# A graph-convolution kernel on one core: the order of the panels in its last step, the place where d is turned, and the order of its loads

## What is computed

```python
h = jnp.maximum(_layernorm(x, axis=-1), 0.0)
rowsum = adj.sum(axis=1)
d_inv_sqrt = jnp.where(rowsum > 0, rowsum ** (-0.5), 0.0)
normalized_adj = d_inv_sqrt[:, None] * adj * d_inv_sqrt[None, :]
support = normalized_adj @ h
out = support @ W + b
x = x + jax.nn.relu(out)
```

## Time and profile before

| | us |
|---|---|
| runs, median of 3 | 409.94 (409.82 to 417.97) |
| profiled execution, its time | 411.25 |
| profiled execution, its span | 409.2 |
| TensorE busy | 390.9 (96%) |
| VectorE busy | 311.0 (76%) |
| ScalarE busy | 292.1 (71%) |
| GpSimd busy | 115.7 (28%) |

### The profile page before, as it was taken

The page is one execution under the profiler, slowest core; times in us unless marked ns, Lnnn a source line. Parts: engine busy times, 40 slices in busy tenths (PEclk is TensorE's granted clock), DMA queues, the critical chain, the costliest instruction groups (busy, mean ns, idle before and its releaser), DMA issues.

```text
span 409.2 us, 5151 instructions
## 1 busy us (share of the span) xinstructions
PE 390.9 (96%) x1760; PEld 324.3 (79%) x1760; DVE 311.0 (76%) x314; ACT 292.1 (71%) x285; POOL 115.7 (28%) x271
## 2 busy tenths in 40 slices
PE   3999799999999999999999999999999999999991
PEld 3888687888888888888888888888888888887771
DVE  5757668878797878869585987869386987929996
ACT  2799868887888888597776778876677793445622
POOL 3343525242422362332132521433023360000000
PEclk9999999999999999999999999999999999999997
DMA  8999999999999999999999989999899991097656
GB/s 286 424 418 362 421 421 422 422 419 421 420 422 422 419 420 421 400 388 425 420 421 361 356 315 389 422 421 422 322 336 360 343 362 70 24 400 295 202 170 243
DMA packets 22472, 147.39 MB, mean 360 GB/s; under 512 B 2608, under 2 KB 2864, under 8 KB 6064
## 3 DMA queue, kind: packets, MB, share of 16 engines
q1 hardware_dynamic: 22448, 147.07, 90.0%
HBM read 142.87 MB, written 4.19 MB: 359 GB/s over the span
## 4 chain that ended last, share of the span: by engine, by line
PE 69%; DMA 12%; DVE 7%; issue 5%; ACT 5%; SPq 1%; ACTq 0%; DVEq 0%
PE moved L685 17%; PE moved L686 17%; PE moved L687 17%; DMA at<-in_adj_t 6%; DMA nat<-in_adj 6%; PE held L685 5%; PE held L686 5%; PE held L687 5%; PE moved L655 3%; DVE acc L551 2%; DVE lo L536 1%; DVE acc L566 1%; DVE nat L572 1%; ACT hi L352 1%; ACT G L364 1%
## 5 line engine op out<-in xcount | busy, mean ns | idle before, releaser
L352 ACT ACTIVATE hi<-at,s 128x1024 fp32r<-128x1024 f32 x112 | 123.0, 1146 | 46.6 <-issue 33.3
L532 DVE SCALAR_TENSOR_TENSOR lo<-at,s,hi 128x1024 fp32r<-128x1024 f32 x112 | 141.1, 1279 | 17.9 <-ACT hi L352 17.9
L685 PE MATMUL moved<-hi,G 128*128 128x512 f32 x384 | 150.1, 391 | 3.0 <-DVE acc L548 2.1
L686 PE MATMUL moved<-lo,G 128*128 128x512 f32 x384 | 149.5, 389 | 0.0
L687 PE MATMUL moved<-hi,G 128*128 128x512 f32 x384 | 149.4, 389 | 0.0
L551 DVE TENSOR_TENSOR acc<-moved,acc 128x1024 f32<-128x1024 f32 x84 | 102.7, 1223 | 53.3 <-PE moved L687 53.2
L339 ACT ACTIVATE nat<-nat 128x2048 f32<-128x2048 f32 x64 | 122.3, 1912 | 12.1 <-DMA nat<-in_adj 12.1
L685 PEld LDWEIGHTS moved<-hi,G 128*128 128x128 f32 x384 | 72.1, 188 | 20.5 <-DVE acc L551 3.2
L687 PEld LDWEIGHTS moved<-hi,G 128*128 128x128 f32 x384 | 72.1, 188 | 15.1
L686 PEld LDWEIGHTS moved<-lo,G 128*128 128x128 f32 x384 | 72.1, 188 | 14.6
L462 POOL TENSOR_TENSOR row_sum<-part 128x1 f32<-128x1 f32 x32 | 16.4, 511 | 170.5 <-ACT nat L339 170.4
(11 more groups left out here) (57 smaller groups left out, 228.4 us busy)
## 6 DMA issues: line engine op xcount, KB each, us to landing
nat<-in_adj SPq DMA_DIRECT2D x64, 1024.0 KB, 10.3
at<-in_adj_t SPq DMA_DIRECT2D x64, 1024.0 KB, 10.6
nat<-in_x_t SPq DMA_DIRECT2D x6, 512.0 KB, 4.1
out<-nat SPq DMA_DIRECT2D x5, 512.0 KB, 5.1
at<-in_x SPq DMA_DIRECT2D x4, 512.0 KB, 5.6
turned<-in_x SPq DMA_DIRECT2D x3, 512.0 KB, 14.1
turned<-in_x_t SPq DMA_DIRECT2D x2, 512.0 KB, 5.2
out<-turned SPq DMA_DIRECT2D x2, 512.0 KB, 5.0
```

The source lines that it names most:

```text
L352: nc.scalar.activation(hi[g % RING][:, 2 * c:2 * c + 2, :], at[g % LA][:, 2 * c:2 * c + 2, :], ACT.Copy, scale=s[:, j:j + 1]).then_inc(hi_ ...
L532: nc.vector.scalar_tensor_tensor(out=lo[g % RING][:, tiles, :], in0=at[g % LA][:, tiles, :], scalar=s[:, j:j + 1], in1=hi[g % RING][:, til ...
L685: nc.tensor.matmul(into[:, f, :], big, hi[g % RING][:, t, :], start=begins, stop=False)
L686: nc.tensor.matmul(into[:, f, :], big, lo[g % RING][:, t, :], start=False, stop=False)
```

## The change

The last step takes the panels in the order 2 to 7, 0, 1, so that both held panels come last. d is turned one step earlier, in step 13, two quarters each within panels 0 and 1 (slot 52), and ScalarE copies it in its loop 52. SP's loop g loads slot g + 3 instead of g + 2, with slot 2 ahead of the loops. The table of row blocks adds one for every 8 slots instead of 13, so `make_G` comes up to two slots earlier. The first chunk of x is loaded in two halves, with a mean for each. In the opening TensorE turns chunk 1 after it has projected chunk 0; ScalarE sums row block 0 before it copies chunk 1; VectorE copies chunks 3 and 4 from PSUM, and centres each chunk before it takes the next one's statistics. x comes back in LX = 4 buffers, and the sum of the first position goes to `acc` like the others.

The core of the diff (left out: declarations of names, `take_stats`, `centre` and `mean_of`, which take the first chunk in halves, and the wait in `project`, which asks `turned_signal`):

```diff
-    return [0] + list(range(HELD, NP)) + [1] if k == LAST else list(range(NP))
+    return list(range(HELD, NP)) + list(range(HELD)) if k == LAST else list(range(NP))
...
-        end = min(2 * WIDTHS[0] + min(2 * (g + 1), g + 3) + g // 13, 2 * NB)
+        end = min(2 * WIDTHS[0] + min(2 * (g + 1), g + 3) + g // 8, 2 * NB)
...
-    LX = 3
+    LX = 4
...
         def x_out(pos):
             e = pos % LX
-            flat = nat[2][:, e * BW * D:(e + 1) * BW * D] if e < 2 else turned[1][:, :]
+            flat = nat[2][:, e * BW * D:(e + 1) * BW * D] if e < 2 else turned[e - 2][:, :]
...
         def total(pos):
-            if pos == 0:
-                return turned[0][:, :].rearrange("p (f r) -> p f r", r=PW)
-            return acc[:, (pos - 1) % (NP - HELD), :, :]
+            return acc[:, pos % (NP - HELD), :, :]
...
+        def turned_signal(c):
+
+            if c in BY_VECTOR:
+                return hT_late, BY_VECTOR.index(c) + 1
+            return hT_ready, c + 1 - sum(b < c for b in BY_VECTOR)
...
-                if pos == 0 and k == LAST:
-                    for q in range(NP // 2):
+                if pos < HELD and k == LAST - 1:
+                    for q in range(2 * pos, 2 * pos + 2):
                         use(("d_row", q), (gathered + q) % ROT, d_row_ready, q + 1)
...
@@ block.sync
-            load_x(0)
+            half = BW // 2
+            sp.dma_start(h(0)[:, 0:half, :], x[0][:, 0:half, :]).then_inc(x_first, DMA)
+            sp.dma_start(h(0)[:, half:BW, :], x[0][:, half:BW, :]).then_inc(x_landed[0], DMA)
             load_x(1)
...
             load_slot(0)
             load_slot(1)
+            load_slot(2)
             sp.dma_start(b_sb[:, :], b).then_inc(b_landed, DMA)
...
-                if g + 2 < len(SLOTS):
-                    load_slot(g + 2)
+                if g + 3 < len(SLOTS):
+                    load_slot(g + 3)
@@ block.scalar
             take_turned(0)
+            sum_nat(0)
             take_turned(1)
-            sum_nat(0)
             round_raw(0)
+            take_turned(2)
             sum_nat(1)
-            take_turned(2)
             sum_nat(2)
             round_raw(1)
-            take_turned(3)
             sum_nat(3)
             round_raw(2)
-            take_turned(4)
             round_slot(0)
...
+                if k == LAST - 1 and q == 0:
+                    for r in range(NP // 2):
+                        take_d_rows(r)
                 if k == LAST:
                     if q == 0:
                         act.wait_ge(b_landed, DMA)
-                        for r in range(NP // 2):
-                            take_d_rows(r)
@@ block.gpsimd
+            def mean_of_first():
+                pool.wait_ge(stats_made, BW // 2)
+                then(nc.gpsimd.tensor_tensor(out=mean2[:, 0:BW // 2], in0=stats[:, 0:BW // 2, 1],
+                                             in1=stats[:, 0:BW // 2, 4], op=ALU.add))
+                nc.gpsimd.tensor_scalar(minus_mean[:, 0:BW // 2], mean2[:, 0:BW // 2], -0.5, None,
+                                        ALU.mult).then_inc(mean_first, 1)
...
-            mean_of(0)
+            mean_of_first()
+            mean_of(0, BW // 2)
             mean_of(1)
+            mean_of(2)
             rstd_of(0)
-            mean_of(2)
@@ block.vector
+            def take_turned(c):
+                dve.wait_ge(h_turned, c + 1)
+                dve.wait_ge(hW_done, c - 1)
+                nc.vector.tensor_copy(hT(c), pair_of(("turn", c))[:, :, :]).then_inc(hT_late, 1)
...
-                if pos == NP - 1:
+                if i < HELD:
                     dve.wait_ge(out_ready, pos - (NP - HELD) + 1)
-                elif i < HELD:
-                    dve.wait_ge(panel_done, NP * LAST + pos + 1)
+                    if pos < NP - 1:
+                        dve.wait_ge(panel_done, NP * LAST + pos + 1)
...
             take_stats(0)
+            centre(0)
             take_stats(1)
-            centre(0)
             centre(1)
             take_stats(2)
+            centre(2)
             take_stats(3)
-            centre(2)
             centre(3)
+            rest_of_raw(0)
             take_stats(4)
-            rest_of_raw(0)
             centre(4)
+            take_turned(3)
             rest_of_raw(1)
+            take_turned(4)
             rest_of_raw(2)
@@ block.tensor
-                    if pos == 0 and c < WIDTHS[k] - 1 and f == FD - 1:
-                        amid(k, c)
+                    if pos < HELD and c == 0 and f == FD - 1:
+                        amid(k, pos)
...
-            def amid(k, c):
+            def amid(k, pos):
...
-                if k == LAST and c >= 1:
-                    turn_d(2 * c - 2)
-                    turn_d(2 * c - 1)
+                if k == LAST - 1:
+                    turn_d(2 * pos)
+                    turn_d(2 * pos + 1)
...
             turn(0)
-            turn(1)
             pe.wait_ge(w_landed, DMA)
             project(0)
+            turn(1)
             turn(2)
```

More of the change, by code:

```diff
@@ L34 @@
 AHEAD = 5
+BY_VECTOR = [3, 4]
 TURNED_IN = {5: 5, 6: 7, 7: 10}
@@ L212, in build @@
         consts_made = sem("consts_made")
+        x_first = sem("x_first")
+        mean_first = sem("mean_first")
         stats_made = sem("stats_made")
@@ L218, in build @@
         hT_ready = sem("hT_ready")
+        hT_late = sem("hT_late")
         hW_done = sem("hW_done")
@@ L247, in use @@
             over[pair] = (signal, count)
+        def turned_signal(c):
+            if c in BY_VECTOR:
+                return hT_late, BY_VECTOR.index(c) + 1
+            return hT_ready, c + 1 - sum(b < c for b in BY_VECTOR)
         for c in range(AHEAD):
-            use(("turn", c), c % ROT, hT_ready, c + 1)
+            use(("turn", c), c % ROT, *turned_signal(c))
         use(("project", AHEAD - 1), AHEAD % ROT, raw_ready, AHEAD)
@@ L258, in build @@
                 if pos == 0 and k in TURNING:
-                    use(("turn", TURNING[k]), gathered % ROT, hT_ready, TURNING[k] + 1)
+                    use(("turn", TURNING[k]), gathered % ROT, *turned_signal(TURNING[k]))
                 if pos == 0 and k in PROJECTING:
@@ L434, in _, with mean_of @@
                                     base=0, pattern=[[-1, P]], channel_multiplier=1).then_inc(consts_made, 1)
-            def mean_of(c):
-                tiles = slice(c * BW, (c + 1) * BW)
+            def mean_of(c, first=0):
+                tiles = slice(c * BW + first, (c + 1) * BW)
                 pool.wait_ge(stats_made, BW * (c + 1))
-                then(nc.gpsimd.tensor_tensor(out=mean2[:, :], in0=stats[:, tiles, 1], in1=stats[:, tiles, 4],
+                then(nc.gpsimd.tensor_tensor(out=mean2[:, first:BW], in0=stats[:, tiles, 1], in1=stats[:, tiles, 4],
                                              op=ALU.add))
-                nc.gpsimd.tensor_scalar(minus_mean[:, tiles], mean2[:, :], -0.5, None,
+                nc.gpsimd.tensor_scalar(minus_mean[:, tiles], mean2[:, first:BW], -0.5, None,
                                         ALU.mult).then_inc(mean_ready, 1)
                 pool.wait_ge(mean_ready, c + 1)
+            def mean_of_first():
[4 more added lines that the diff above has]
+                                        ALU.mult).then_inc(mean_first, 1)
             def rstd_of(c):
@@ L494, in take_stats @@
             def take_stats(c):
-                dve.wait_ge(x_landed[c % AHEAD], DMA * (c // AHEAD + 1))
                 for t in range(BW):
+                    if c == 0 and t == 0:
+                        dve.wait_ge(x_first, DMA)
+                    if t == (BW // 2 if c == 0 else 0):
+                        dve.wait_ge(x_landed[c % AHEAD], DMA * (c // AHEAD + 1))
                     nc.vector.bn_stats(stats[:, c * BW + t, :], h(c)[:, t, :]).then_inc(stats_made, 1)
             def centre(c):
-                dve.wait_ge(mean_ready, c + 1)
                 for t in range(BW):
                     j = BW * c + t
+                    if c == 0 and t == 0:
+                        dve.wait_ge(mean_first, 1)
+                    if t == (BW // 2 if c == 0 else 0):
+                        dve.wait_ge(mean_ready, c + 1)
                     nc.vector.tensor_scalar(h(c)[:, t, :], h(c)[:, t, :], minus_mean[:, j:j + 1], 0.0,
                                             ALU.add, ALU.max).then_inc(h_ready, 1)
+            def take_turned(c):
+                dve.wait_ge(h_turned, c + 1)
+                dve.wait_ge(hW_done, c - 1)
+                nc.vector.tensor_copy(hT(c), pair_of(("turn", c))[:, :, :]).then_inc(hT_late, 1)
             def rest_of_raw(c):
@@ L649, in project @@
                     pe.wait_ge(raw_ready, c - 1)
-                pe.wait_ge(hT_ready, c + 1)
+                signal, count = turned_signal(c)
+                pe.wait_ge(signal, count)
                 for a in range(2):
@@ L705, in turn_d @@
                 mm.then_inc(d_turned, 1)
-            def amid(k, c):
-                if k in TURNING:
```

(12 more changed lines are left out.)

## The result

The changed kernel takes 406.79 us (median of 8 runs, 405.96 to 408.4) against 409.88 for the kernel before (8 runs): a ratio of 0.9917, 95% interval 0.9896 to 0.9939. It is 3.1 us faster by the medians, clear of noise and under 2%. (The ratio is estimated from the runs in the fast state alone, so it is not the quotient of the two medians.) The profiled execution took 406.59 us, its span is 404.7.

The account below looks back on a forecast made before the run. TensorE, busy 96% of the span, was taken as the bound, plus its waits, start and end. Last step and end -5.1 and the part before -0.1 made -5.2 us: 404.7 us against the median, range 402.4 to 407.7.

Parts of the forecast that it names:

- first rival: Before the last step: the transfers give the gain back, up to +2.6 us, 407.4 us; 20%.
- Last step and end: From T, the start of slot 56: waits of 2.1 us go and the end shortens by 3.0, together -5.1 us.
- 3.0 us of it: End: VectorE finishes 2.7 us instead of 5.70 behind the last matmul's start, a gain of 3.0 us.
- third rival: Last step: VectorE's 5.88 us loops start late, slot 60 held by loads of x; 2.1 us stay, 406.8; 8%.
- The opening: Before slot 0: project(1) waits for the copy behind the first row sum until 16.0; slot 0 at 31.4, +0.5 us.
- the rival of 4%: Opening: TensorE's clock stays at its lower level through the gaps; slot 0 is 6.6 us late, 411.4 us; 4%.
- the sum up to slot 52: Everything up to the last step: opening +0.5 and slots 0 to 10 -0.6, together -0.1 us.
- slots 0 to 10: First slots: a shorter early wait, -1.1, against longer later waits, +0.5, together -0.6 us.
- the -1.1 for the wait at 46.96: Early slots: row block 7 lands at 39.7 to 40.9, so TensorE waits 1.0 to 1.4 us instead of 2.3.
- the +0.5 for later waits: Near 65 to 85 us: waits of 0.8 instead of 0.3 us, +0.5, bounds 0 and +3.

Follow-up runs that it names:

- e4: The kernel before, run again unchanged for a second profile: ratio 1.0006, median 410.12 us; its profiled execution took 409.87 us.
- e9: The kernel before with only the table of row blocks changed, one more every 8 slots instead of 13: ratio 0.9921, 406.10 us.
- e10: The kernel before with only the slot loads one slot further ahead (distance 3), old table: ratio 0.9956, 407.61 us.
- e6: The changed kernel with idle transposes of the identity on TensorE, 18 before turn(0) and 6 behind it: 0.9897 against the kernel before, 406.87 us.
- e5: The changed kernel with the opening of before: 0.9906 against the kernel before, 406.81 us.
- before 2: The second profile of the unchanged kernel before, taken in e4: profiled execution 409.87 us.
- e3: The kernel before with only the new opening: ratio 1.0023, 411.36 us.
- e1: The changed kernel with the old opening and slot loads at the old distance 2: 0.9887 against the kernel before, 405.64 us.
- e11: The kernel before with table divisor 8 and d turned in step 13, panels in the old order: ratio 0.9922, 406.20 us.
- e12: The changed kernel with slot loads at the old distance 2: 0.9920 against the kernel before, 406.36 us.
- e2: The kernel before with slot loads at distance 3 and table divisor 8, old opening and last step: ratio 0.9930, 407.32 us.
- e8: The changed kernel with slot 3 rounded before row blocks 6 and 7 are summed: 0.9906 against the kernel before, 407.18 us.
- e7: As e6, with ScalarE copying chunk 1 before it sums row block 0: 0.9950 against the kernel before, 408.76 us.

## Why the prediction was right, and where it was off

**The direction and the range** held: 406.79 lies in 402.4 to 407.7, and the forecast was 404.7. The size was 3.1 us, not 5.2. That the time lies inside the range is owed to the room that the first rival made on the slow side, up to 407.4, and not to the sum. Two things make up the 2.1 us. The span of the profiled executions fell by 409.2 - 404.7 = 4.5 us: 0.7 less than 5.2, since slot 52 started 1.2 us later than I had summed (+1.1 for -0.1) and 0.5 more was gained behind it (5.6 for 5.1). The other 1.4 are the reference: I took the terms from an execution 1.4 us over the median, as if a shift between executions were spread evenly. It was not. e4 shows that 1.0 of it was early waits and 0.8 waits of the last step, and part of these I had booked as gains.

**Last step and end: -5.1 forecast, -5.6 measured.** Slots 5.44 us apart, VectorE's loops from T + 8.3 (8.2 forecast), its end 2.60 behind the last matmul (2.7), slot 52 longer by 3.5: each as written, and 0.4 in the stores on top. The cause, though, I had given in two halves, and one was idle. I credited 3.0 us of it to panels 0 and 1 coming last without gathers. e9 gets 2.5 of those 3.0 with the old order, by loading slot 59 earlier. VectorE's 5.88 us a loop against 5.44 had room for its loops once they started on time (T + 11.2 in e9, T + 15.9 before); the slope I read in the earlier trace rows was real, but the late start behind the wait in the earlier trace rows was what made it bind. e10, which frees slot 59 in another way, shows the same. The third rival (it doesn't do what it says) fell: slot 60 behind the loads of x was never late.

**The opening: +0.5 forecast, +1.15 measured, and the reason was wrong.** I had `project(1)` held by the copy behind the first row sum until 16.0. It started at 16.57, and the copy had waited 0.40 us for TensorE. What held it was `project(0)`, 5.53 us long, ten of its matmuls at the lower clock level. The level had not fallen in the gap of 1.19 us: it had been the lower one since the first transpose, and it rose only near 12.9 us, where it rose near 11.9 in the profile before although TensorE had started 1.3 us later. I had named the gap and priced it only as the rival of 4%, all or nothing; a part of it came true. e6 shows the clock as the cause, and e5 that the lateness cost little at the end. Why the level rose later here than before, no run tells.

**The step furthest off is the sum up to slot 52: -0.1 forecast, +1.1 measured** (+2.1 against the second profile). Opening and slots 0 to 10 together were to bring slot 11 to 93.67 + 0.5 - 0.6 = 93.57; it started at 94.39. First matmul of slot 11, before and changed:

```profile
93.67 0.39 PE L685 MATMUL moved<-hi,G 128*128 128x512 f32 x1
...
94.39 0.39 PE L718 MATMUL moved<-hi,G 128*128 128x512 f32 x1
```

That is 0.8 of the 1.2 us; the other 0.4 come between slots 11 and 52, 236.5 us long against 236.2 and 236.5 in the two profiles of before. The term that failed is the -1.1 for the wait at 46.96: it shrank by 0.3. I had let row block 7 land at 39.7 to 40.9; ScalarE found it at 42.2. The hole in the transfers was filled (from 362 to 421 GB/s in the fourth slice of the page) and row block 7 came late all the same, for the change puts each slot ahead of its row block in the queue, and ScalarE needs both. Against the +0.5 for later waits, the one at 69.06 went (-0.3) and one of 0.2 came in slot 10. So slots 0 to 10 gave 0.4 where I had summed 0.6, by two misses that nearly cancel, and the opening, 0.65 over, is the larger miss by that count. But the terms do not add, as the starts of slots 0 and 11 in all profiles show:

| divisor, distance | kernels | slot 0 | slot 11 |
|---|---|---|---|
| 13, 2 | before, before 2, e3 | 30.90, 30.64, 32.19 | 93.67, 92.31, 95.34 |
| 13, 3 | e10 | 31.30 | 93.44 |
| 8, 2 | e1, e9, e11, e12 | 30.87, 30.87, 30.22, 31.74 | 92.84, 93.33, 92.65, 93.73 |
| 8, 3 | e2, e5, changed, e8, e6 | 30.99, 30.66, 32.05, 32.45, 32.97 | 94.32, 94.09, 94.39, 94.67, 94.41 |
| 8, 3 | e7 (clock lower at 50 us) | 30.83 | 97.64 |

With the divisor 8 and distance 3 slot 11 comes near 94.4 wherever slot 0 was; at distance 2 it comes about 1 us earlier and a late opening is still seen in it. These are single profiles, and those of before differ by 1.4 us at slot 11, so the price of the distance stays near 1 us by the profiles and unproven by the times (see e12). The first rival described this and held it at 20%, up to +2.6 before the last step; 1.1 of it came true. The extra row block of loop 8 shows in slot 10, which takes 5.44 us in the four profiles with divisor 13 and 5.6 to 6.5 in the nine of divisor 8 other than e7: 0.2 to 1.1 us, around the +0.5 I had summed for later waits.

**What stays open.** The wait near 47 us varies by 1 us between executions of one kernel (2.2 and 1.2 in the two profiles of before). It goes with when row blocks 6 and 7 and slot 3 land, and no run here tells why their landing varies.

## What to carry to other kernels

A wait at the head of a queue of loads can show up three engines further on: here the queue waited, then ScalarE's rounding, VectorE's `lo` and TensorE came late. The cheapest cure was one constant that made the last G two slots earlier, and it was worth as much as the whole change. When two streams share a queue and a consumer needs one of each, moving one ahead can make the other late, as row block 7 here; ask which of them lands last, not how far ahead the queue runs. Before summing a gain from waits in one profile, look at a second execution: waits of the stage bound by transfers differed by 1 us between two of them, a third of what the change brought.

## What was not expected of the hardware

TensorE's clock starts at its lower level, and in one run it fell back to it after a wait of less than 2 us. In all fourteen profiles the first transposes start 0.21 us apart, and 0.11 once the level has risen. In the changed kernel nothing fell back in the opening; the level only rose late, near 12.9 us, within `project(0)`. In e6 it rose near 6.1 us, and `project(0)` ran at full speed (0.22 us a matmul). Then TensorE waited 1.77 us, and eight matmuls of `project(1)` started 0.43 us apart. Stretches of e6, the granted clock in the third column from the right:

```profile
16.00:18.00 2.00, 2.00 (x6) 1.60 (x6) 2.00 (x5) 2.00 (x3) 0.00 (x0) 0.59 1.03 418
18.00:20.00 2.00, 2.00 (x7) 1.61 (x6) 1.46 (x5) 2.00 (x3) 0.30 (x2) 0.56 1.00 418
```

In the stream of the slots waits of 2.50 us (e5) and 2.74 us (e3) left it at full speed, and one of 3.24 us, in e7, was followed by matmuls at 0.43 us, with a granted clock of 0.58 in the stretch from 50 to 52 us. 0.56 to 0.59 lie between the shares of the two levels, 1.2 and 2.4 GHz, because the fall or the rise lies in the stretch. So the length of the wait alone does not tell in these runs whether the level falls. Ahead of the first rise the granted clock stood at 1.00 in the profiles of before, the changed kernel, e3, e6 and e7, where the distances of the transposes show the lower level; there they are the better witness. The Trainium skill, "TensorE: Matmul & The Clock Gate", Part 1, calls the throttled state the default and says that activity releases it; the traces agree, since every kernel here meets that default at its start.
